# Packing each expert's weights into one transfer, with a new interleaving of the steps, in an eight-image pipeline on one core

## The chip, the core and the metric

The kernel runs on one core of a Trainium2 chip, in one launch. The metric is the device time in microseconds (us). Five engines work side by side, each through its own program: TensorE (PE in the profile; PEld is its weight load), VectorE (DVE), ScalarE (ACT), GpSimd (POOL) and SyncE (SP), which here issues the plain transfers. They wait for each other by counting semaphores, which the program sets and reads explicitly.

## What is computed

Eight images of 32 x 32 tokens and 128 channels, all in fp32, go through six layers with a residual each:

```
x = x + deformable_conv(group_norm(x))       # 9 taps, 4 corners each, gathered at computed places
x = x + sort_over_tokens(corr(group_norm(x)))[ranks]   # 1024 x 1024 correlations, 128 ranks of the sorted row
t = t + windowed_attention(layer_norm(t))    # windows of 4, 16 and 32
u = layer_norm(t)
t = t + u + sum_e g[:, e] * (gelu(u @ w1[e] + b1[e]) @ w2[e] + b2[e])   # 8 experts of 128 x 128, top 2
t = t + state_space_scan(layer_norm(t))
u = layer_norm(t)
h = silu(u @ w1[e].T) * (u @ w3[e].T)        # 8 experts, hidden size 341, top 2
t = t + sum_e g[:, e] * (h @ w2[e].T)
```

The experts are computed for all tokens, and the gate g is zero where a token does not use one. The experts of 128 x 128 are called moe1, those with hidden size 341 moe2 or the last layer.

## The kernel before

**Pipeline.** A body of the program works on several images at once: the first part (F: group norm, deformable convolution with its gathers, correlations) of image i+1, the sort (S, VectorE alone) of image i, and the rest of the layers (C: attention, moe1, scan; M: moe2) of images i-1 and i in halves of 512 tokens. The bodies are called fill, early, full, late and drain by what runs in them; there are six full bodies (i = 1 to 6), and in the drain only C and M are left.

**Order.** Each engine's program is one interleaving of the generators F, S, C and M. The function weave (L1697) goes through a string of letters and lets the generator of that letter write its next step. There is one string for each engine and kind of body in ORDER (L44 and on), `DVE_full`, `PE_full` and so on. A step's instructions stand in the engine's queue where its letter stands, so a letter moved is an instruction moved ahead of or behind others, whatever is ready first.

**Gathers.** pool_F (L748 to L761) issues the gathers of a deformable convolution in groups of three indirect DMAs (L758) into one of two halves of `gath`; group g is issued when the matmuls of group g-2 have freed its half. The matmuls (L597) take 12 gathered 128 x 128 tiles times diagonal weights; each fp32 matmul appears twice in the trace, so 12 instructions are x24 there. L604, L605 and L607 are the convolution proper of a finished tile of 128 tokens (residual, bias, 9 taps).

**Sort.** Comparison stages on 128 x 1024 values twice (L791 and L793 among others), and at the end the selection stages (L901), which keep only the ranks that are wanted; L910 adds the result.

**moe1.** SyncE's sp_C (L956 to L965) loads w1 and w2 of an expert with two DMAs of 64 KB into one of three slots of `e1w`; TensorE's pe_moe1 (L1179 to L1205) waits for them. The layer norm behind it starts with the statistics at L933.

**Scan.** L1316, L1317 (decays), L1332, L1334, L1338 (TensorE's products of a chunk), L1516 (VectorE takes the result), L1344 and L1350 (transposes and output projection), L1530 (VectorE adds it to `tm`).

**moe2.** sp_M (L1537 to L1553) loads an expert's weights with five DMAs into one of two slots of `e2w`: w1 and w3 whole, and w2 in three tiles of 128, 128 and 85 rows. Expert e may be loaded when all of e-2 has been used (`y2_ps`). On TensorE (pe_M) an expert is 3 tiles of its hidden size, 128, 128 and 85. Each tile has u @ w1 (L1605, with `mu_t`), (g u) @ w3 (L1610, with `gated_u`), and, a tile later, the product with w2 (L1590). L1581 makes the gated input of the next expert. ScalarE takes the silu of L1605's result (L1658), VectorE multiplies it with L1610's (L1690), and L1590 uses that. Two banks (MB) alternate between the results, so TensorE can be only about one result ahead of its readers.

## Time and profile before

| | us |
|---|---|
| timed runs | 4749.79, 4736.45, 4748.96; median 4748.96 |
| the profiled execution | 4740.47 |
| its span, first to last instruction | 4738.7 |

Engines over the span: TensorE busy for 3969.3 us (84%) in 20178 instructions, VectorE 4160.9 us (88%) in 5173, ScalarE 3082.4 us (65%) in 7523, GpSimd 940.8 us (20%) in 580. TensorE's granted clock is 0.916 of the full one on average. The chain of work that ended last is 48% VectorE, 34% TensorE, 7% issue, 4% ScalarE, 4% DMA and 3% GpSimd. DMA moves 269.67 MB, 57 GB/s on average.

To read it: fill and early last until 959 us, the six full bodies until 4157 us (each about 532 us), the late body until 4440 us and the drain until the end. Busy shares over the whole span mix these; a stretch is read by its own rows. An idle time in front of an instruction is printed behind it with the engine, tile and line that ended it.

### The profile page before, as it was taken

How to read it: one execution, taken by the hardware profiler on the slowest of the kernel's cores; microseconds unless marked ns; L12 is line 12 of the kernel's file. 1: busy time of each engine (PE TensorE's matmuls, PEld its weight loads, DVE VectorE, ACT ScalarE, POOL GpSimd, SP SyncE). 2: the span in 40 equal slices, each digit the busy share in tenths (PEclk: the TensorE clock that was granted, in tenths of full speed). 3: DMA queues.
4: the chain of work that ended last, by engine and by line, in shares of the span. 5: the costliest groups of instructions: out<-in, count | busy, mean ns of one | idle time of the engine just before them, and what ended most of it. 6: DMA issues, size and time to landing. Idle time of an engine off the chain costs nothing.

```text
span 4738.7 us, 57761 instructions
## 1 busy us (share of the span) xinstructions
PE 3969.3 (84%) x20178; PEld 2730.7 (58%) x20178; DVE 4160.9 (88%) x5173; ACT 3082.4 (65%) x7523; POOL 940.8 (20%) x580
## 2 busy tenths in 40 slices
PE   5756648989889998988989998989889998768787
PEld 3636434676557754676557755676557755544554
DVE  1099999999999999999999999999999999999421
ACT  4536526777668856777668856777568856455562
POOL 2327000341006300351005400341005300000000
PEclk8878869999999999999999999999999999888898
DMA  4323101232023311232013211232023210000001
GB/s 139 102 56 116 29 0 31 73 95 60 19 58 101 86 33 32 76 93 59 19 51 107 83 36 26 75 96 62 20 56 103 86 28 19 18 21 24 28 28 32
DMA packets 227492, 269.67 MB, mean 57 GB/s; under 512 B 27900, under 2 KB 189956, under 8 KB 227076
## 3 DMA queue, kind: packets, MB, share of 16 engines
q0 software_dynamic: 46080, 151.03, 11.0%
q1 hardware_dynamic: 181124, 114.95, 8.6%
q8 instruction: 162, 2.65, 0.2%
q14 instruction: 126, 1.03, 0.1%
HBM read 242.54 MB, written 23.34 MB: 56 GB/s over the span
## 4 chain that ended last, share of the span: by engine, by line
DVE 48%; PE 34%; issue 7%; ACT 4%; DMA 4%; POOL 3%; SPq 1%; DVEq 0%; POOLq 0%; ACTq 0%
PE bank L597 9%; DVE srt_b L846 4%; DVE srt_b L830 4%; DVE srt_a L791 3%; DVE srt_a L793 3%; PE bank L1610 3%; PE bank L1605 3%; DMA gath<-quads,idx 3%; PE bank L1590 3%; POOL gath L758 3%; DVE srt_a L868 3%; DVE srt_b L793 3%; DVE srt_a L858 3%; DVE srt_a L866 2%; DVE act L1690 2%
## 5 line engine op out<-in xcount | busy, mean ns | idle before, releaser
L758 POOL DMA_INDIRECT gath<-quads,idx x576 | 940.6, 1633 | 2844.3 <-DVE idx L722 1942.4
L597 PE MATMUL bank<-diag,gath 128*128 128x128 f32 x4608 | 610.9, 296 | 149.4 <-DMA gath<-quads,idx 149.3
L639 ACT ACTIVATE diag<-ident,w 128x128 f32<-128x128 f32 x2304 | 703.4, 394 | 27.3 <-DVE w L737 27.2
L597 PEld LDWEIGHTS bank<-diag,gath 128*128 128x128 f32 x4608 | 594.7, 211 | 187.9 <-DMA gath<-quads,idx 165.9
L1590 PEld LDWEIGHTS bank<-e2w,act 128*128 128x128 f32 (+1 forms) x3072 | 426.7, 205 | 172.3 <-issue 169.3
L1610 PE MATMUL bank<-gated_u,e2w 128*128 128x512 f32 (+1 forms) x768 | 434.9, 650 | 91.3 <-DVE act L1690 88.7
L1605 PE MATMUL bank<-mu_t,e2w 128*128 128x512 f32 (+1 forms) x768 | 432.6, 647 | 73.9 <-DMA e2w<-moe_w_t 54.0
L1690 DVE TENSOR_TENSOR act<-act,bank 128x512 f32<-128x512 f32 (+1 forms) x384 | 261.0, 680 | 196.4 <-PE bank L1610 163.1
L1590 PE MATMUL bank<-e2w,act 128*128 128x128 f32 (+1 forms) x3072 | 428.7, 288 | 1.5 <-DVE act L1690 1.5
L830 DVE TENSOR_TENSOR srt_b<-srt_a 128x1024 f32<-128x1024 f32 (+3 forms) x208 | 370.8, 1783 | 2.8
L1658 ACT ACTIVATE act<-bank 128x512 f32<-128x512 f32 (+1 forms) x384 | 228.5, 595 | 207.0 <-PE bank L1605 202.8
L846 DVE TENSOR_TENSOR srt_b<-srt_a 128x1024 f32<-128x1024 f32 x192 | 350.6, 1826 | 0.0
L1658 ACT ACT_TABLE_LOAD x223 | 286.1, 1283 | 6.4 <-PE bank L1590 2.6
L1610 PEld LDWEIGHTS bank<-gated_u,e2w 128*128 128x128 f32 (+1 forms) x768 | 132.3, 191 | 248.7 <-issue 236.5
L791 DVE TENSOR_TENSOR srt_a<-srt_b 128x2048 f32<-128x2048 f32 x112 | 256.0, 2286 | 0.8
L793 DVE TENSOR_TENSOR srt_a<-srt_b 128x2048 f32<-128x2048 f32 x112 | 255.8, 2284 | 0.0
L672 ACT ACTIVATE cols<-bank 128x384 f32<-128x384 f32 x192 | 92.0, 483 | 250.4 <-PE bank L597 242.0
L791 DVE TENSOR_TENSOR srt_b<-srt_a 128x2048 f32<-128x2048 f32 x96 | 219.5, 2286 | 1.1
L793 DVE TENSOR_TENSOR srt_b<-srt_a 128x2048 f32<-128x2048 f32 x96 | 219.2, 2283 | 0.0
L866 DVE TENSOR_TENSOR srt_a<-srt_b 128x2016 f32<-128x2016 f32 (+1 forms) x96 | 211.6, 2204 | 0.6
L868 DVE TENSOR_TENSOR srt_a<-srt_b 128x2016 f32<-128x2016 f32 (+1 forms) x96 | 211.7, 2205 | 0.0
L1605 PEld LDWEIGHTS bank<-mu_t,e2w 128*128 128x128 f32 (+1 forms) x768 | 122.8, 189 | 137.8 <-DMA e2w<-moe_w_t 67.0
(339 smaller groups left out, 8101.5 us busy)
## 6 DMA issues: line engine op xcount, KB each, us to landing
e2w<-moe_w_t SPq DMA_DIRECT2D x256, 170.5 KB
quads<-xn_tok SPq DMA_DIRECT2D x128, 128.0 KB, 2.5
e1w<-L_ffn_w SPq DMA_DIRECT2D x256, 64.0 KB
e2w<-moe_w_t SPq DMA_DIRECT2D x256, 64.0 KB
gath<-quads,idx POOLq DMA_INDIRECT x576
e2w<-moe_w_t SPq DMA_DIRECT2D x128, 42.5 KB
x_tok<-x SPq DMA_DIRECT2D x8, 512.0 KB, 4.0
out<-tm SPq DMA_DIRECT2D x16, 256.0 KB, 2.5
```

The costliest lines, as they stand in the source:

```text
L597: ins = T.matmul(FB[q % 2][:, k * P:(k + 1) * P], gath[:, g % 2, k, s * C:(s + 1) * C], diag[:, g % 2, 4 * k + s], start=(s == 0), stop=(s ...
L639: ins = SC.activation(diag[:, g % 2, n], ident[:], ACT.Copy, scale=w[:, n:n + 1])
L758: pool.indirect_dma_start(gath[:, g % 2, k], None, quads, bass.IndirectOffsetOnAxis(idx[:, TG * g + k:TG * g + k + 1], 0)).then_inc(sem["g ...
L791: V.tensor_tensor(dst[:, :, 0:size // 2], lo, hi, ALU.max)
L793: return V.tensor_tensor(dst[:, :, size // 2:size], lo, hi, ALU.min)
L830: V.tensor_tensor(out_lo, lo, hi, ALU.max)
L846: link.put(V.tensor_tensor(out_hi, lo, hi, ALU.min))
L1590: ins = T.matmul(MB[2][:, t * P:(t + 1) * P], act2[0:m, n % ACT2_SLOTS, t * P:(t + 1) * P], e2w[0:m, e % 2, W2 + k * C:W2 + (k + 1) * C], ...
L1605: T.matmul(MB[r % 2][0:m, :], e2w[:, e % 2, k * P:k * P + m], mu_t[:], start=True, stop=True).then_inc(sem["m_ps"], 1)
L1610: T.matmul(MB[r % 2][0:m, :], e2w[:, e % 2, W3 + k * P:W3 + k * P + m], gated_u[:], start=True, stop=True).then_inc(sem["m_ps"], 1)
L1658: SC.activation(act2[0:m, n % ACT2_SLOTS], MB[r % 2][0:m, :], ACT.Silu).then_inc(sem["m_sb"], 1)
L1690: V.tensor_tensor(act2[0:m, n % ACT2_SLOTS], act2[0:m, n % ACT2_SLOTS], MB[r % 2][0:m, :], ALU.mult).then_inc(sem["hh"], 1)
```

## The change

Three things change together.

The weights of a moe1 expert lie side by side in one array `moe1_w_t` (8 x 128 x 256) and come with one DMA of 128 KB instead of two of 64 KB. The weights of a moe2 expert lie in one array `moe2_w_t` (8 x 128 x 1066, w1, w3 and w2 with its last tile filled up to 128 rows by zeros) and come with one DMA of 533 KB, 4264 bytes for each of 128 partitions, instead of five with 511.5 KB together. The semaphores that count them go up by 16 an expert instead of 32 and 80. Slots, and the points from which a load may start, stay.

The strings of ORDER are new for the early, full, late and drain bodies, for all engines. The steps themselves are the same. In the changed file the lines of moe2 carry numbers that are 5 lower (L1600, L1605, L1585 and L1576 for L1605, L1610, L1590 and L1581; L1685 for L1690), those of the scan 1 lower (L1343 and L1349 for L1344 and L1350, L1529 for L1530).

```diff
@@ ORDER, one line of a table of some seventy @@
     SP_full=(
-        "CCCMMCMCCCCFFCCCMMMMMMMMMCCCCMCMFMMMM"
+        "CCCMMMFCCFCCCCCCMMMMMMMMMCMCCCCMMFMMM"
     ),
@@ semaphores @@
-            e1_in0=96, e1_in1=96, e1_in2=64, logit=1, ...
+            e1_in0=48, e1_in1=48, e1_in2=32, logit=1, ...
-            e2_in0=80 * 4, e2_in1=80 * 4, gate_diag=E8, ...
+            e2_in0=16 * 4, e2_in1=16 * 4, gate_diag=E8, ...
@@ sp_C @@
-                sp.dma_start(e1w[:, e % E1_SLOTS, 0], A["L2_ffn_w1"][e]).then_inc(sem["e1_in%d" % (e % E1_SLOTS)], 16)
-                sp.dma_start(e1w[:, e % E1_SLOTS, 1], A["L2_ffn_w2"][e]).then_inc(sem["e1_in%d" % (e % E1_SLOTS)], 16)
+                sp.dma_start(e1w[:, e % E1_SLOTS].rearrange("p a c -> p (a c)"), A["moe1_w_t"][e]).then_inc(sem["e1_in%d" % (e % E1_SLOTS)], 16)
@@ pe_moe1 @@
-                    pe.wait_ge(sem["e1_in%d" % (n % E1_SLOTS)], unit("e1_in%d" % (n % E1_SLOTS), i, h, 32 * (n // E1_SLOTS + 1)))
+                    pe.wait_ge(sem["e1_in%d" % (n % E1_SLOTS)], unit("e1_in%d" % (n % E1_SLOTS), i, h, 16 * (n // E1_SLOTS + 1)))
@@ sp_M @@
-                sp.dma_start(e2w[:, e % 2, 0:HID], A["moe2_w1_t"][e]).then_inc(sem["e2_in%d" % (e % 2)], 16)
-                sp.dma_start(e2w[:, e % 2, W3:W3 + HID], A["moe2_w3_t"][e]).then_inc(sem["e2_in%d" % (e % 2)], 16)
-                for k, m in enumerate(HTILES):
-                    sp.dma_start(e2w[0:m, e % 2, W2 + k * C:W2 + (k + 1) * C],
-                                 A["moe2_w2_t"][e, k * P:k * P + m]).then_inc(sem["e2_in%d" % (e % 2)], 16)
+                sp.dma_start(e2w[:, e % 2], A["moe2_w_t"][e]).then_inc(sem["e2_in%d" % (e % 2)], 16)
@@ pe_M @@
-                        pe.wait_ge(sem["e2_in%d" % (e % 2)], unit("e2_in%d" % (e % 2), i, h, 80 * (e // 2 + 1)))
+                        pe.wait_ge(sem["e2_in%d" % (e % 2)], unit("e2_in%d" % (e % 2), i, h, 16 * (e // 2 + 1)))
@@ layouts @@
+    w2 = np.zeros((E8, len(HTILES) * P, C), np.float32)
+    w2[:, 0:HID] = a["L3_ffn_w2"].transpose(0, 2, 1)
+    w2 = w2.reshape(E8, len(HTILES), P, C).transpose(0, 2, 1, 3).reshape(E8, P, len(HTILES) * C)
+    packed = np.concatenate([a["L3_ffn_w1"].transpose(0, 2, 1), a["L3_ffn_w3"].transpose(0, 2, 1), w2], 2)
```

**TensorE in a full body, around the eighth expert of moe2 for the first half.** `gated_u,e2w` and `mu_t,e2w` are the two products of a tile, `diag,gath` a gather group, `e2w,act` the product with w2, `cols` the convolution. Before:

```order
L597 MATMUL bank<-diag,gath 128x128 x12
L1605 MATMUL bank<-mu_t,e2w 128x512
L1610 MATMUL bank<-gated_u,e2w 128x512
L1590 MATMUL bank<-e2w,act 128x128 x4
L597 MATMUL bank<-diag,gath 128x128 x12
L1605 MATMUL bank<-mu_t,e2w 128x512
L1610 MATMUL bank<-gated_u,e2w 128x512
L1590 MATMUL bank<-e2w,act 128x128 x4
L1605 MATMUL bank<-mu_t,e2w 85x512
L597 MATMUL bank<-diag,gath 128x128 x12
L1610 MATMUL bank<-gated_u,e2w 85x512
```

After, from the end of the first tile on:

```order
L1605 MATMUL bank<-gated_u,e2w 128x512
L1585 MATMUL bank<-e2w,act 128x128 x4
L1600 MATMUL bank<-mu_t,e2w 128x512
L604 MATMUL bank<-x_tok,ident 128x128
L605 MATMUL bank<-conv_bias,ident 128x128
L607 MATMUL bank<-conv_w,cols 128x128 x9
L597 MATMUL bank<-diag,gath 128x128 x12
L1343 MATMUL bank<-ident,arena 128x128 x8
L1605 MATMUL bank<-gated_u,e2w 128x512
L1585 MATMUL bank<-e2w,act 128x128 x4
L1600 MATMUL bank<-mu_t,e2w 85x512
L1349 MATMUL bank<-w_out,arena 128x128 x8
```

Behind these stand L597 x24 (two gather groups) and the last tile's L1605 (85x512). The convolution and the first of the three gather groups, which stood ahead of the expert's first tile, now stand behind it, with the scan's transposes and projection between the second tile's and the third's.

**VectorE at the same place.** `act<-act,bank` is the product of a tile; `srt_a`, `srt_b` are the sort's buffers. Before:

```order
L1690 TENSOR_TENSOR act<-act,bank 128x512
L791 TENSOR_TENSOR srt_b<-srt_a 128x256x8
L793 TENSOR_TENSOR srt_b<-srt_a 128x256x8
L1690 TENSOR_TENSOR act<-act,bank 128x512
L901 TENSOR_TENSOR srt_a<-srt_b 128x4x53x4
L901 TENSOR_TENSOR srt_a<-srt_b 128x4x75x4
L1690 TENSOR_TENSOR act<-act,bank 85x512
L933 BN_STATS mst<-tm 128x6 x4
L941 BN_AGGR mmv<-mst 128x2 x4
L901 TENSOR_TENSOR srt_b<-srt_a 128x4x11x2
```

After, from the second tile's product to the third's (the first tile's stands seven rows above these):

```order
L1685 TENSOR_TENSOR act<-act,bank 128x512
L901 TENSOR_TENSOR srt_a<-srt_b 128x4x53x4
L901 TENSOR_TENSOR srt_a<-srt_b 128x4x75x4
L901 TENSOR_TENSOR srt_b<-srt_a 128x4x11x2
L901 TENSOR_TENSOR srt_b<-srt_a 128x4x42x2
L901 TENSOR_TENSOR srt_b<-srt_a 128x4x43x2
L901 TENSOR_TENSOR srt_b<-srt_a 128x4x32x2
L901 TENSOR_TENSOR srt_a<-srt_b 128x4x11
L901 TENSOR_TENSOR srt_a<-srt_b 128x4x21 x2
L901 TENSOR_TENSOR srt_a<-srt_b 128x4x22
L901 TENSOR_TENSOR srt_a<-srt_b 128x4x21 x2
L901 TENSOR_TENSOR srt_a<-srt_b 128x4x11
```

The third tile's product (L1685, 85x512) stands right behind these: it follows three selection stages now and one before. Between the first tile's product and the second's there are now two pairs of comparisons (L791, L793) and the projection's sum (L1529), where there was one pair.

**TensorE in a full body, where the scan of the first chunk meets the gathers.** Before:

```order
L1590 MATMUL bank<-e2w,act 128x128 x4
L1332 MATMUL bank<-arena,ident 128x256
L1334 MATMUL bank<-arena 128x32 x8
L1338 MATMUL bank<-carry,arena 128x256
L1605 MATMUL bank<-mu_t,e2w 128x512
L597 MATMUL bank<-diag,gath 128x128 x12
L1610 MATMUL bank<-gated_u,e2w 128x512
L1590 MATMUL bank<-e2w,act 128x128 x4
L597 MATMUL bank<-diag,gath 128x128 x12
```

After:

```order
L1605 MATMUL bank<-gated_u,e2w 128x512
L1585 MATMUL bank<-e2w,act 128x128 x4
L1600 MATMUL bank<-mu_t,e2w 85x512
L597 MATMUL bank<-diag,gath 128x128 x12
L1315 MATMUL bank<-future_h,ident_h 128x512
L1316 MATMUL bank<-tbu,later 128x512
L1315 MATMUL bank<-future_h,ident_h 128x512
L1316 MATMUL bank<-tbu,later 128x512
L1331 MATMUL bank<-arena,ident 128x256
L1333 MATMUL bank<-arena 128x32 x8
L1337 MATMUL bank<-carry,arena 128x256
```

The products of the scan's first chunk (L1332 to L1338 before, L1331 to L1337 now) stood behind one gather group of the image and stand behind three now.

## Rows read from the trace of the kernel before

**Rows 1.** Windows: busy us (and instructions) of each engine, three stretches.

```profile
1491.40:2023.00 531.60, 482.38 (x2523) 333.47 (x2522) 517.69 (x646) 385.74 (x943) 121.36 (x72) 0.95 0.22 62
4640.00:4738.70 98.70, 74.85 (x323) 47.40 (x322) 14.41 (x21) 23.67 (x52) 0.00 (x0) 0.88 0.12 35
4695.50:4709.50 14.00, 10.83 (x45) 6.62 (x46) 2.06 (x3) 3.55 (x8) 0.00 (x0) 0.87 0.13 37
```

The columns are the stretch, its length, the busy time of PE, PEld, DVE, ACT and POOL, then the granted clock, the busy share of the DMA engines and GB/s.

**Rows 2.** Waits of VectorE, 959 to 4157: us in total, times, longest.

```profile
DVE act L1690 <- PE bank L1610: 43.5, 16, 7.3
...
DVE msd L1676 <- ACT msd L1622: 5.3, 6, 1.0
DVE lnst L933 <- ACT td L1236: 1.3, 4, 0.4
```

**Rows 3.** Timeline, 1470 to 1506, by engine: start us, us, what, idle before.

```profile
1484.75 1.12 DVE L1530 SCALAR_TENSOR_TENSOR tm<-bank,rms,td 128x128 f32<-128x128 f32 x4
...
1490.18 0.68 DVE L1690 TENSOR_TENSOR act<-act,bank 128x512 f32<-128x512 f32 x1
...
1495.79 2.35 DVE L901 TENSOR_TENSOR srt_a<-srt_b 128x848 f32<-128x848 f32 x2
1504.83 0.68 DVE L1690 TENSOR_TENSOR act<-act,bank 85x512 f32<-85x512 f32 x1 [6.69 <-PE bank L1610]
...
1477.58 2.17 PE L607 MATMUL bank<-conv_w,cols 128*128 128x128 f32 x18
...
1481.37 2.84 PE L597 MATMUL bank<-diag,gath 128*128 128x128 f32 x24
...
1484.91 1.02 PE L1610 MATMUL bank<-gated_u,e2w 128*128 128x512 f32 x2
...
1498.29 5.49 PE L597 MATMUL bank<-diag,gath 128*128 128x128 f32 x24 [4.44 <-DMA gath<-quads,idx]
...
1485.01 0.94 POOL L758 DMA_INDIRECT gath<-quads,idx  x1 [4.35 <-PE bank L597]
1486.26 4.83 POOL L758 DMA_INDIRECT gath<-quads,idx  x1 [0.30 <-issue]
1491.39 4.70 POOL L758 DMA_INDIRECT gath<-quads,idx  x1 [0.30 <-issue]
```

**Rows 4.** Waits of TensorE, 4640 to 4738.7.

```profile
PE bank L1605 <- DMA e2w<-moe_w_t: 20.3, 6, 3.8
```

**Rows 5.** Timeline, 4718 to 4726, SyncE's issues (SPq) and TensorE.

```profile
4718.88 0.33 SPq L1542 DMA_DIRECT2D e2w<-moe_w_t  x1
...
4719.73 1.28 SPq L1545 DMA_DIRECT2D e2w<-moe_w_t  x3
...
4722.83 2.08 PE L1605 MATMUL bank<-mu_t,e2w 128*128 128x512 f32 x2 [3.15 <-DMA e2w<-moe_w_t]
...
4724.70 1.67 PE L1610 MATMUL bank<-gated_u,e2w 128*128 128x512 f32 x2
```

**Rows 6.** The page's DMA issues: count, KB each, median us to landing.

```profile
x_tok<-x SPq DMA_DIRECT2D x8, 512.0 KB, 4.0
out<-tm SPq DMA_DIRECT2D x16, 256.0 KB, 2.5
```

**Rows 7.** Timeline of TensorE behind two shorter waits.

```profile
771.17 1.10 PE L1605 MATMUL bank<-mu_t,e2w 128*128 128x512 f32 x2 [2.14 <-DVE act L1690]
...
2466.49 1.98 PE L1610 MATMUL bank<-gated_u,e2w 128*85 128x512 f32 x2 [2.17 <-DVE act L1690]
```

**Rows 8.** Timeline of VectorE behind rows 3: the two small selection stages.

```profile
1506.54 1.42 DVE L901 TENSOR_TENSOR srt_b<-srt_a 128x88 f32<-128x88 f32 x4
1507.99 1.49 DVE L901 TENSOR_TENSOR srt_a<-srt_b 128x44 f32<-128x44 f32 x7
```

**Rows 9.** Timeline of GpSimd at the third gather group of an image.

```profile
1956.56 1.41 POOL L758 DMA_INDIRECT gath<-quads,idx  x1 [8.10 <-PE bank L597]
...
1960.41 2.90 POOL L758 DMA_INDIRECT gath<-quads,idx  x1 [0.31 <-issue]
```

More of the change, by code:

```diff
@@ L74 @@
     ),
     SP_full=(
-        "CCCMMCMCCCCFFCCCMMMMMMMMMCCCCMCMFMMMM"
+        "CCCMMMFCCFCCCCCCMMMMMMMMMCMCCCCMMFMMM"
+    ),
+    DVE_full=(
+        "CMSSCMSSSSSMSSMSSSCCMSSCCMSSMSSSMSSSSSSCSSSCMSSMSSCMFCFCSSCFMCSSCFMSSSSSMSSSSMSSSSMSSSSSSSSSCMSS"
+        "CSSMSSSSSSSSSCSSCMSSCMSSCFSSCFMCCFFMSSCFSSSCMSSCSSMSSCMSSSSCCMSSCSSCMSSCMSSCMSSSSCMSSCSSCMSSSMMS"
+        "SSCMSSSCSSMSSMSSSMSSMSSCCMSSSCMCSSSSSSSSSSSCMSSCMSSMSSCSSSCMSSCMSSCMSSCSSCMSSMSSSSSMSSSSMSSSSSSM"
+        "SSSCMSSCSSSSMSSSSCSSCMSSCSSSCMSSCMSSCCMSSCFFMCFSSCFMSSFSSCMSSCMSSCSSCMSSCMSSCMCSSCSSCSSCSS"
@@ new lines @@
+        "MFMCFMMMCCMFFFMFFFFFFMFCMMCMFFFFFFCCMCFFFCMCCFMMFFFCMCFFFMFFFFFMMFCCFFFCFMFFFFFFFFMMFFFMCFMCFFFM"
+        "CFFCCCFFCFFFCCCMCCFMFFCFMCFFFCFMMFFFCFMFCFFMCFFMCMMFFFFFFMFFFMFFFFFFMFFMMCCMCCMCCCCMCCCCCCCCMMCM"
+        "CMCFFFFCMCCFFMMCFCCFFCCCCCCCCMCFMFMFMMMFCCMFMFMMFCCMFFCCMCFMCMCMCFCCFMFCCFCFFFFF"
+    ),
+    SP_late=(
+        "CCCMMMCMCCCCCCCMMMMMMMMCCMCCCMMMMM"
+    ),
+    ACT_late=(
+        "MCFFFMCMFCCCMCFCFFCCFCCFFCMCCCMMFCMMCFMFCMCMMMMMMMMCCMCCMCCCCMCCCCCCCCMMCMCMCCMCMMCCCCCCCCCCCCMM"
+        "CMMMMCCMMMMCCMCCMCCMCMCCMCCCCMMMMCCMCCCCCCCCCMCCCCMMCMMCCMCMMMMMMCCMCCMMCMCCCCCMMCCCCCCMMCMCMCCM"
+        "CCMMCCCCCCCCCCCMMCMMMMCCMMMMCCMCCMCMCMCMCCCMCCC"
@@ L115 @@
+        "MSSCSSSSSMSSSSSSCSSCMSSCMSSCSSSCMSSCCMSSCMSSCSSCMSSSSCMSSCMSSCSSCCSSMSSCCMSSCSSCMSCSMSMSSSCSSCMS"
+        "SSMSSMSSSCCMSSCCMSSMSSSSSSSSSCSSSCMSSMSSCSSCMSSCSSSCMSSCMSSCMSSSSMSSSSSMSSMSSSSMSSSSMSSCMSSSCSSS"
+        "SMSSSSCSSCMSSCMSSCSSSCMSSCCMSSCMSSCSSCMSSSSCMSSCMSSCSSCMSSCMSSCMCSSCSSCSSSCS"
     ),
     DVE_drain=(
-        "MCMCMMMMMMCCMCCMCMCMMCCCCCCMMMMMMCMCCCMMCMCCCCCCMCMCMCCCMCMCCMCCMMCMMMMMMMMMMMMMMMMMMMMMMMMMMMMM"
+        "MCMCMMMMMMCCMCMMCMMCMCCCCCCCMMMMMCMCCCMCMMCCCCCCCMCMMCCMMCCMCCMCCMCMMMMMMMMMMMMMMMMMMMMMMMMMMMMM"
@@ L323, in build @@
             expd=2, probd=2, prob_ps=2, prob_sb=2, ctx_ps=1, ctx_sb=1, att_out=1, t1=1,
-            e1_in0=96, e1_in1=96, e1_in2=64, logit=1, g_e=1, g_exp=1, gated=1, gt_ps=1, gt_sb=1, h_ps=E8, gelu=E8, gy=E8, y1_acc=E8,
+            e1_in0=48, e1_in1=48, e1_in2=32, logit=1, g_e=1, g_exp=1, gated=1, gt_ps=1, gt_sb=1, h_ps=E8, gelu=E8, gy=E8, y1_acc=E8,
             y1_ps=E8, t2=1,
@@ L1842, in layouts @@
         w_out_t=t(a["L3_attn_W_out"].T.reshape(2, P, C).transpose(1, 0, 2)),
-        moe2_w1_t=t(a["L3_ffn_w1"].transpose(0, 2, 1)), moe2_w3_t=t(a["L3_ffn_w3"].transpose(0, 2, 1)),
-        moe2_w2_t=t(a["L3_ffn_w2"].transpose(0, 2, 1)),
+        moe1_w_t=t(np.concatenate([a["L2_ffn_w1"], a["L2_ffn_w2"]], 2)), moe2_w_t=t(packed),
   )
```

62 lines of the change are left out of this document (21 added, 41 removed).

## Prediction

> **What bounds the kernel now.** I read the stretches first. A middle body of the pipeline lasts 531.6 us, and VectorE is busy for 517.7 us of it, TensorE for 482.4 us [rows 1]. So VectorE sets the pace of the six full bodies, and only 13.9 us of each can be won; the sorting and the other VectorE work is not touched by the change. In the last 98.7 us it is the other way round: VectorE is busy for 14.4 us, TensorE for 74.9 us [rows 1], and the chain goes load, matmul, evacuation, product. These are the two places where the change can act.
>
> Next the waits of VectorE in the full bodies. One group stands out: the product of an expert of the last layer (L1690) waits for TensorE's L1610, 43.5 us in 16 waits, the longest 7.3 us [rows 2]. That is one wait of about 6.7 us in each of the six full bodies and little else. The next group is 5.3 us in 6 waits, 0.9 us a body [rows 2]. The timeline shows what it is made of [rows 3]. TensorE has done the matmuls of one gather group at about 1484.2. That frees the buffer, and GpSimd issues the three indirect DMAs of the group after the next: 0.94 us, then 4.83 and 4.70 us, each beside a pair of long VectorE comparisons. The data are there at 1498.29, the 24 matmuls take 5.49 us because TensorE has stood still and its granted clock is down, and only behind them comes the L1610 on which VectorE has waited since about 1498.1. From freed buffer to VectorE's product it is 1504.8 - 1484.2 = 20.6 us, and VectorE had 13.9 us of other work to cover it.
>
> Last the waits of TensorE in the last stretch: 20.3 us in 6 waits for the load of the expert's weights [rows 4]. Each expert needs its own load, the slot is free only when the expert before the last is done, and nothing else is left to run.
>
> **The change, part by part.**
>
> Fewer issues. An expert of the last layer costs SyncE one issue instead of five, one of moe1 one instead of two. SyncE waits nearly all the time, and in the full bodies the loads are under VectorE's work, so the saved issues give nothing there by themselves: 0 us. The one bigger transfer moves 533 KB instead of 511.5 KB (zeros pad the last tile), which the DMA engines, 13% busy in the sixth expert's cycle [rows 1], don't feel.
>
> The last stretch. Now the first issue starts at 4718.88, the third kind, three issues in 1.28 us, at 4719.73, so the very last issue at about 4720.7, and TensorE goes on at 4722.83 [rows 5]: 3.95 us from the first issue, of which 1.8 us pass until the last issue and 2.1 us from there. This wait is 3.15 us and the mean of the six 3.4 us, so the mean from first issue to matmul is 4.2 us. With one transfer the 1.8 us of issuing go, but all the data then stand behind one issue. Upper bound: 2.1 us and all of the data behind it; the share of the DMA engines in the sixth expert's cycle, 0.13 of 14.0 us, says 1.8 us for 16 engines [rows 1], so 3.9 us. Lower bound: 256 KB land 2.5 us after their issue; 512 KB land after 4.0 us, though among the gathers of a full body [rows 6]. I take 3.4 us, nearer to the middle of the two since part of the 2.1 us is the tail of the earlier transfers. That is 0.8 us for each of six loads: **-4.8 us** (0.3 to 1.7 us each, so -1.8 to -10). The Trainium skill, "DMA: Bandwidth & Descriptors", "Anatomy of one DMA", fits 2.0 us plus bytes over 436 GB/s for one DMA from the GpSimd path, which is an estimate of 3.25 us here and would give 0.95 us each, 5.7 us in all; the trace agrees with its fixed part (2.1 us for the 42.5 KB at the end).
>
> Then the clock. Behind such a wait of 3.15 us the next matmuls run at half clock: L1605 takes 2.08 us and L1610 1.67 us [rows 5] where they take 1.02 us otherwise [rows 3], 1.7 us lost for each load. The wait would become 2.6 us on average. Behind waits of 2.14 and 2.17 us the clock held once (1.10 us) and fell once (1.98 us) [rows 7], so I count a fifth of 6 x 1.7 us: **-2 us**, from 0 to -10.
>
> The rest of the drain, 4440 to 4640, where the experts of the first half run beside the scan of the second: TensorE waits for scalars and the scan and hardly for weights. The new order groups moe1's experts more tightly there. I give it **-2 us**, and 8 us either way, because a step moved by one tile costs or gives about one tile (2.6 us) and there are a few of them.
>
> The wait in the full bodies. The order moves both sides of it (the pieces of TensorE and VectorE above). On VectorE the last product now stands behind the two small selection groups, 1.42 and 1.49 us [rows 8], so it is wanted 2.9 us later. On TensorE the convolution and the first of three gather groups now stand behind L1605 of the first tile and not ahead of it, so the buffer is freed later: about 0.9 for the products, 0.9 for the next gate, 2.4 for the convolution and 2.7 for the gather's matmuls, 6.9 us behind the first tile's L1605 (L1610 before the change), which ends 4 to 5 us ahead of its product on VectorE (1485.9 against 1490.18, [rows 3]); so some 2 us behind that product. From that product VectorE now has 16.5 us of work to the last one (four comparisons of 2.2 us, the projection's 1.1 us, two products of 0.6 us and 5.3 us of selection), where it had 8 us. That leaves 14.5 us of cover for what took 20.6 us, against 13.9 us. So 0.6 us is sure if the gather takes as long as now. It may be quicker, since its third DMA now falls beside selection and not beside comparisons; without any blocking three issues take under 4 us instead of 11.1 us, and the half clock of 5.49 us may go too. I take 2.5 us of the 6.7 us in each of six bodies: **-15 us**, between -40 (the wait is gone) and 0.
>
> The Trainium skill, "SBUF — State Buffer", "SBUF: two separate sides", says that the ports shared by VectorE and GpSimd are an exclusive lock, and that descriptors written by GpSimd starve while VectorE holds it. By it the length of the comparisons and not the DMA sets the 4.8 us, which the rows bear out (4.83 and 4.70 beside comparisons, 0.94 else); the new order keeps those comparisons in front of the gather, and if both middle DMAs stayed blocked the term above would be 6 times 0.6, -4 us.
>
> New waits. Beside the big wait VectorE waits for little more than 1 us in most full bodies [rows 2], so the old order fitted; the new one moves some hundred steps. The tightest that I find: moe1's eight experts have to run in about 38 us of VectorE's work where they had 47 us before (my sum of the rows between the gates and the next statistics; TensorE's rows in it sum to 35 us), and the wait of the statistics (L933) for it is 1.3 us in 4 waits now [rows 2]. A second is the projection (L1530): TensorE's L1350 for it now stands behind 12 us of matmuls after the first tile's gate, and VectorE asks for it 9.5 us after the first tile's product, which leaves 2 us. I take **+8 us** for six bodies, 0 to +40 for its range.
>
> Sum: -4.8 - 2 - 2 - 15 + 8 = -16 us. The profiled execution took 4740.5 us (span 4738.7 us and 1.8 us around it), so it would be 4724.5 us. The three timed runs lie at 4736.5, 4749.0 and 4749.8 us; the profiled one is 8.5 us under their median. I put the base in the middle, 4744.7 us, and forecast **4728 us**. Against the runs a difference of 0.3% (14 us) is about what can be told from no change.
>
> **The rivals.**
>
> A gather that blocks the scan (slower). In the new order the third gather group of an image stands ahead of TensorE's L1332 to L1338 for the first chunk, whose result VectorE wants at L1516; in the old one it stood behind them. Its DMAs take 1.41 to 2.90 us each now, done 7 us after their start [rows 9], and then the new order has some 2 us of slack by my sums. If they are blocked as those of rows 3 were, 11 us instead of 7, VectorE waits 2 us, and with the half clock behind it 5 to 6 us. It decides from a delay of 2 us. Six bodies give +33 us on top of the forecast without its +8: 4744.7 - 24 + 33 = 4754 us at least, and 4765 us if the old wait stays as well. For it: the same lock. Against it: at that place GpSimd ran at 1.4 to 2.9 us in the old order.
>
> The middle doesn't move. The gather's blocking and the new waits cancel what VectorE's new cover gives, and only the last 100 us get better: -5 to -9 us, 4738 us. For it: the cover grows by only 0.6 us if the gather stays as slow.
>
> The wait goes. The gather is issued between the comparisons, all six waits of 6.7 us go (-40 us), and the drain gives 8 more: 4697 us. For it: the product is wanted 2.9 us later; against it: the chain was 6.7 us late.
>
> The packed load is no faster. If 533 KB behind one issue take the upper 3.9 us or more, the last stretch gives 0 to 2 us. Then the whole is at 4736 us.
>
> **How the numbers follow.** Forecast (middle gains 4 to 12 us, drain the rest): 43%. Middle unmoved: 24%. Wait gone: 13%. Blocked scan: 14%. Load no faster: 6%. Faster by over 0.3%: three quarters of the forecast and the case without the wait, 46%. Slower by over 0.3%: the blocked scan and a little of the middle case, 17%. Within: 37%. The range leaves out the far ends of the two extreme cases, 4696 to 4764 us.
>
> **What would show it.** One SyncE issue per expert, and TensorE's waits for weights in the last stretch at 2.6 us instead of 3.4 us, six of them; L1605 behind them at 2.08 us or 1.1 us tells the clock term. VectorE's wait for the last tile's gated product: 4 us instead of 6.7 us in each full body, with GpSimd's DMAs just ahead of it. VectorE busy for the same 517.7 us in a body whose length drops from 531.6 to about 530 us. The forecast is wrong if a wait of VectorE for the scan's product, or for moe1's output, of some us shows in each body; or if the load takes as long as before.

## The result and the profile after

The changed kernel is slower: 4798.1 us (median of four runs, 4793.0 to 4802.1) against 4743.8 us of the kernel before (median of four, 4736.5 to 4749.8). The ratio is 1.012, with a 95% interval of 1.0102 to 1.0139, so +54 us where the prediction said -16 us. The profiled execution took 4802.1 us, span 4800.3 us.

Where the time went is read from stretches first. A middle body, from one add of the ranks (L910) to the same add a body later, and the last 98.7 us, in windows of the changed kernel (stretch, length, busy time of PE, PEld, DVE, ACT, POOL, granted clock, DMA share, GB/s):

```profile
2064.74:2606.80 542.06, 484.03 (x2525) 333.95 (x2524) 518.17 (x646) 380.07 (x937) 130.99 (x73) 0.95 0.21 61
...
4701.60:4800.30 98.70, 78.51 (x338) 49.34 (x338) 15.79 (x23) 26.40 (x59) 0.00 (x0) 0.89 0.12 36
```

VectorE has as much to do as before (518.2 us against 517.7 us in [rows 1]), and the body is 10.5 us longer. Five of the six bodies read alike: 542.3, 540.3, 542.1, 542.7 and 542.6 us. From the adds of the ranks, the six bodies together take 3239.4 us where they took 3185.3 us: 54.1 us, with 52.4 us of it idle time of VectorE and 1.7 us busy time. The front grew by 4.9 us and the end by 2.6 us, which makes the 61.6 us between the two spans.

What VectorE waits for in the middle, 959 to 4200 us of the changed kernel (us in total, times, longest):

```profile
DVE act L1685 <- ACT act L1653: 46.5, 6, 7.8
DVE arena L1515 <- PE bank L1337: 28.1, 10, 4.4
DVE arena L1113 <- PE bank L1004: 14.9, 5, 3.2
DVE arena L1510 <- ACT arena L1421: 5.6, 5, 1.1
DVE lnsd L1052 <- ACT lnsd L1042: 3.7, 6, 0.6
DVE act L1685 <- PE bank L1605: 2.1, 6, 0.8
```

The old wait is gone altogether: the last group fell from 43.5 us to 2.1 us [rows 2]. The place that rows 3 showed reads now, on the timeline (start us, us, what, idle before):

```profile
2594.46 2.09 POOL L758 DMA_INDIRECT gath<-quads,idx  x1 [0.30 <-issue]
...
2601.14 2.95 PE L597 MATMUL bank<-diag,gath 128*128 128x128 f32 x24 [0.47 <-DMA gath<-quads,idx]
...
2605.05 0.68 DVE L1685 TENSOR_TENSOR act<-act,bank 85x512 f32<-85x512 f32 x1
```

No DMA of GpSimd stands for 4.8 us there, TensorE waits 0.47 us for the gather instead of 4.44 us, its matmuls take 2.95 us instead of 5.49 us, and VectorE's last product starts on time. But five groups of waits stand above it now, four of them of 5 us or more. Of these four the old list had one of over 0.2 us, and that in a single body. The largest, at the first product of an expert:

```profile
2155.22 5.25 POOL L758 DMA_INDIRECT gath<-quads,idx  x1 [0.30 <-issue]
...
2155.64 2.84 PE L597 MATMUL bank<-diag,gath 128*128 128x128 f32 x24
2165.27 5.49 PE L597 MATMUL bank<-diag,gath 128*128 128x128 f32 x24 [6.79 <-DMA gath<-quads,idx]
2170.55 1.25 PE L1600 MATMUL bank<-mu_t,e2w 128*128 128x512 f32 x2
...
2172.35 0.58 ACT L1653 ACTIVATE act<-bank 128x512 f32<-128x512 f32 x1
...
2172.96 0.69 DVE L1685 TENSOR_TENSOR act<-act,bank 128x512 f32<-128x512 f32 x1 [7.82 <-ACT act L1653]
```

It is the old wait over again at another place. The twentieth gather group stands right behind the nineteenth and ahead of the expert's L1600. GpSimd's DMA stands for 5.25 us, TensorE waits 6.79 us for the data and then runs at half clock for 5.49 us, ScalarE's silu comes after both, and VectorE waits 7.82 us. The second place, at the scan's result:

```profile
2531.79 1.02 PE L1600 MATMUL bank<-mu_t,e2w 128*85 128x512 f32 x2
2537.68 5.49 PE L597 MATMUL bank<-diag,gath 128*128 128x128 f32 x24 [4.87 <-DMA gath<-quads,idx]
...
2547.39 0.69 PE L1337 MATMUL bank<-carry,arena 32*128 32x256 f32 x2
...
2524.61 4.60 POOL L758 DMA_INDIRECT gath<-quads,idx  x1 [0.31 <-issue]
2529.52 5.80 POOL L758 DMA_INDIRECT gath<-quads,idx  x1 [0.30 <-issue]
...
2548.12 0.42 DVE L1515 TENSOR_TENSOR arena<-bank,ecum 128x256 f32<-128x256 f32 x1 [4.12 <-PE bank L1337]
```

This is the rival of the blocked gather as the prediction described it: the third group ahead of the scan's first products, its last two DMAs of 4.6 and 5.8 us, half clock behind the wait. With the two waits that follow from it, 1.5 us at the next chunk's L1515 and 1.1 us at L1510, it costs 6.7 us a body. The list has it for five bodies; in the first full body it stands before 959, at 923 to 934, again 6.7 us, and so is in what the front grew by. The third is small:

```profile
2086.37 0.58 ACT L1059 ACTIVATE u_t<-bank 128x512 f32<-128x512 f32 x1
...
2087.00 3.78 PE L989 MATMUL bank<-u_t,wqkvo 128*128 128x512 f32 x4 [3.32 <-ACT u_t L1059]
...
2097.00 1.16 DVE L1113 TENSOR_TENSOR arena<-bank,band 128x960 f32<-128x960 f32 x1 [2.56 <-PE bank L1004]
```

ScalarE copies the attention's input late (behind the copy of a late gather group, four diagonals and a table load), and TensorE's chain to the scores is late by 2.6 to 3.2 us.

In the last stretch the loads went nearly as forecast: TensorE waits for weights six times, 16.6 us in all. SyncE's issue (SPq) and TensorE, and the page's line for the load:

```profile
4780.84 0.33 SPq L1541 DMA_DIRECT2D e2w<-moe_w_t  x1
...
4784.40 1.12 PE L1600 MATMUL bank<-mu_t,e2w 128*128 128x512 f32 x2 [2.76 <-DMA e2w<-moe_w_t]
4785.36 1.66 PE L1605 MATMUL bank<-gated_u,e2w 128*128 128x512 f32 x2
```

```profile
e2w<-moe_w_t SPq DMA_DIRECT2D x128, 533.0 KB, 3.6
```

From issue to matmul it is 3.56 us, where the five issues took 3.95 us [rows 5] and 4.2 us on average.

### The profile page after: what moved, and what is told of

It is laid out like the page before. It is cut to its first block, busy times and chain, and to the rows that moved or that the text cites. A ratio compares the mean times of both kernels' runs of the same rounds, so it can differ in the third digit from the quotient of the medians.

```text
span 4800.3 us, 57083 instructions
## 1 busy us (share of the span) xinstructions
PE 4007.2 (83%) x20178; PEld 2744.0 (57%) x20178; DVE 4163.3 (87%) x5173; ACT 3038.7 (63%) x7479; POOL 991.8 (21%) x580
## 4 chain that ended last, share of the span: by engine, by line
DVE 45%; PE 33%; issue 6%; ACT 6%; POOL 5%; DMA 4%; SPq 0%; DVEq 0%; POOLq 0%; ACTq 0%
PE bank L597 7%; POOL gath L758 5%; DVE srt_b L846 4%; DVE srt_b L830 4%; DMA gath<-quads,idx 4%; DVE srt_a L858 3%; PE bank L1585 3%; DVE srt_a L868 3%; DVE srt_a L791 3%; PE bank L1605 3%; DVE srt_a L793 3%; DVE srt_a L866 3%; PE bank L1600 2%; DVE act L1685 2%; DVE srt_b L858 2%
## 5 line engine op out<-in xcount | busy, mean ns | idle before, releaser
L758 POOL DMA_INDIRECT gath<-quads,idx x576 | 991.6, 1722 | 2866.6 <-DVE idx L722 1909.2
L597 PE MATMUL bank<-diag,gath 128*128 128x128 f32 x4608 | 630.6, 301 | 187.2 <-DMA gath<-quads,idx 182.4
L597 PEld LDWEIGHTS bank<-diag,gath 128*128 128x128 f32 x4608 | 610.0, 215 | 217.6 <-DMA gath<-quads,idx 196.8
L1585 PEld LDWEIGHTS bank<-e2w,act 128*128 128x128 f32 (+1 forms) x3072 | 419.5, 202 | 166.1 <-issue 164.3
L1600 PE MATMUL bank<-mu_t,e2w 128*128 128x512 f32 (+1 forms) x768 | 427.3, 639 | 70.9 <-DMA e2w<-moe_w_t 43.5
L1605 PE MATMUL bank<-gated_u,e2w 128*128 128x512 f32 (+1 forms) x768 | 434.1, 649 | 58.6 <-DVE act L1685 54.0
L1585 PE MATMUL bank<-e2w,act 128*128 128x128 f32 (+1 forms) x3072 | 423.5, 286 | 0.0
L1685 DVE TENSOR_TENSOR act<-act,bank 128x512 f32<-128x512 f32 (+1 forms) x384 | 261.3, 681 | 182.9 <-PE bank L1605 123.3
L830 DVE TENSOR_TENSOR srt_b<-srt_a 128x1024 f32<-128x1024 f32 (+3 forms) x208 | 370.6, 1782 | 2.6 <-issue 0.3
L1653 ACT ACTIVATE act<-bank 128x512 f32<-128x512 f32 (+1 forms) x384 | 227.6, 593 | 205.3 <-PE bank L1600 202.8
L846 DVE TENSOR_TENSOR srt_b<-srt_a 128x1024 f32<-128x1024 f32 x192 | 350.8, 1827 | 0.0
L1605 PEld LDWEIGHTS bank<-gated_u,e2w 128*128 128x128 f32 (+1 forms) x768 | 134.4, 192 | 226.3 <-issue 202.4
L791 DVE TENSOR_TENSOR srt_a<-srt_b 128x2048 f32<-128x2048 f32 x112 | 256.0, 2286 | 1.1
L793 DVE TENSOR_TENSOR srt_a<-srt_b 128x2048 f32<-128x2048 f32 x112 | 255.8, 2284 | 0.0
L791 DVE TENSOR_TENSOR srt_b<-srt_a 128x2048 f32<-128x2048 f32 x96 | 219.6, 2288 | 0.8
L793 DVE TENSOR_TENSOR srt_b<-srt_a 128x2048 f32<-128x2048 f32 x96 | 219.4, 2285 | 0.0
L1600 PEld LDWEIGHTS bank<-mu_t,e2w 128*128 128x128 f32 (+1 forms) x768 | 122.0, 189 | 130.6 <-issue 61.0
```

The source lines that it names most:

```text
L597: ins = T.matmul(FB[q % 2][:, k * P:(k + 1) * P], gath[:, g % 2, k, s * C:(s + 1) * C], diag[:, g % 2, 4 * k + s], start=(s == 0), stop=(s ...
L758: pool.indirect_dma_start(gath[:, g % 2, k], None, quads, bass.IndirectOffsetOnAxis(idx[:, TG * g + k:TG * g + k + 1], 0)).then_inc(sem["g ...
L791: V.tensor_tensor(dst[:, :, 0:size // 2], lo, hi, ALU.max)
L793: return V.tensor_tensor(dst[:, :, size // 2:size], lo, hi, ALU.min)
L830: V.tensor_tensor(out_lo, lo, hi, ALU.max)
L846: link.put(V.tensor_tensor(out_hi, lo, hi, ALU.min))
```

## The experiments

Every experiment was compared with runs of the kernel before on the same chip; their medians lay between 4734 and 4742 us, and not all experiments ran on one chip, so times of different experiments are compared with care (the intervals of the ratios are 10 to 25 us wide). The names g3, g9, g11, g20 stand for the third, ninth, eleventh and twentieth gather group of an image (of 24).

**The two halves of the change.** One run takes the changed kernel and the old table:

```diff
-ORDER = dict( ... the new strings ... )
+ORDER = dict( ... the strings of the kernel before ... )
```

> The changed kernel with the order strings of the kernel before: the packed loads alone. Theory (the order costs all of the +54 us, the packed loads give a little in the last stretch): TensorE's six waits for weights in the last 100 us sum to about 16.6 us instead of 20.3 us, VectorE keeps its wait of 6.7 us for the last gated product in each full body, periods stay 532 us, and the whole is 3 to 6 us below the kernel before, ratio 0.999. Rival (the packed loads disturb the gathers or the other transfers): periods of full bodies grow by some us and the whole comes out at 4755 us or more.

Measured: 4734.0 us, ratio 0.9987 (0.9977 to 0.9998). VectorE's waits in the middle are nearly those of before (39.9 us in 15 for L1605, and one of 6.6 us for L1653 in two bodies), and the last stretch reads:

```profile
PE bank L1600 <- DMA e2w<-moe_w_t: 16.7, 6, 2.9
```

The packed loads alone give 6.4 us (4740.3 us for the kernel before on that chip), 1 to 11 us by the interval of the ratio: at the edge of what can be measured, as the theory had it. The other run takes the kernel before and the new table:

```diff
-ORDER = dict( ... the strings of the kernel before ... )
+ORDER = dict( ... the new strings ... )
```

> The kernel before with the new order strings: the order alone, five and two loads for each expert. Theory (order): periods of 542 us, VectorE waits 7.8 us for the first silu of an expert (L1658), 5.7 us for the scan's product (L1516) and 3 us for the attention's scores in each full body, the whole at about 4802 us, 4 us over the changed kernel, ratio 1.013. Rival (the packed loads or both together are needed for the loss): below 4760 us.

Measured: 4802.8 us, ratio 1.0137 (1.0121 to 1.0152), with the same waits as the changed kernel (46.4 us, 29.4 us and 15.3 us in the three groups). The order costs all of it, and the transfers are not to blame.

**The ends of the pipeline.** The new strings in the full bodies only:

```diff
-    PE_early=( new ), PE_late=( new ), PE_drain=( new ), ... the same for DVE, ACT and SP
+    PE_early=( old ), PE_late=( old ), PE_drain=( old ), ... the same for DVE, ACT and SP
     PE_full=( new ), DVE_full=( new ), ACT_full=( new ), SP_full=( new ),
```

> The changed kernel with the new strings in the full bodies alone; the early, late and drain bodies have those of the kernel before. Theory (the full bodies carry the loss, the other strings cost some 5 us in the drain): periods of 542 us as in the changed kernel, and the stretch behind the last ranked half takes 317 us instead of 322 us, so the whole is 5 to 10 us below the changed kernel, 4788 to 4793 us. Rival (the new strings of the bodies at the ends gain what was hoped for, and more is lost in the full bodies): the whole is at 4798 us or above.

Measured: 4785.7 us, ratio 1.010 (1.0074 to 1.0126), 12.4 us below the changed kernel, a little more than expected. The stretch behind the last add of the ranks takes 316.7 us, as with the old strings and packed loads (316.9 us), where the changed kernel needs 322.3 us and the kernel before 321.3 us. So the loads give 4.4 us there and the new order takes 5.4 us back. The other traces bear out that there is such a cost beside packed loads (322.2 to 322.5 us with the new strings, 313.0 to 318.7 us with the old), but with the loads of before the new strings cost nothing there (321.6 against 321.3 us). The steps from run to run are -6.4 us for the loads, +51.7 us for the full bodies' order (4785.7 against 4734.0) and +12.4 us for the ends. The second is far outside the noise and the first barely; the last is not settled, since the intervals of the two ratios overlap (1.0102 to 1.0139 and 1.0074 to 1.0126).

**g3 behind the scan.** In the changed kernel one letter of TensorE's string moves, and two of ScalarE's, so that the copy behind g3 doesn't hold the next decay (L1421):

```diff
     PE_full=( ...
-        "...MCMFMMMFCCMMMF..."
+        "...MCMFMMMCCMFMMF..."
     ACT_full=( ...
-        "...MMCMFFFFFFCCMC..."
+        "...MMCMFFFFCFFCMC..."
```

> The changed kernel with one gather group moved: in TensorE's full body the third gather group stands behind the scan's first products and the last gated product instead of ahead of them, and on ScalarE the copy that follows it stands behind the next decay. Theory (TensorE stands still in front of the blocked gather while VectorE waits for the scan): VectorE's waits for the scan (L1515, 5.7 us, and L1510, 1.1 us) fall under 1 us in each full body, the periods fall from 542.3 us to about 535.6 us, the whole from 4798 us to about 4761 us. Rival (the scan's chain itself is late): the wait stays at 4 us or more, the whole stays within 10 us of 4798 us.

Measured: 4753.4 us, ratio 1.0028 (1.0015 to 1.0041): 44.7 us won by one move. The waits in the middle, and the place (timeline):

```profile
DVE act L1685 <- ACT act L1653: 44.1, 6, 7.9
DVE arena L1113 <- PE bank L1004: 9.2, 3, 3.2
...
DVE arena L1515 <- PE bank L1337: 0.8, 1, 0.8
```

```profile
2518.76 0.69 PE L1337 MATMUL bank<-carry,arena 32*128 32x256 f32 x2
2519.38 1.09 PE L1605 MATMUL bank<-gated_u,e2w 128*85 128x512 f32 x2
2520.31 2.84 PE L597 MATMUL bank<-diag,gath 128*128 128x128 f32 x24
...
2505.54 4.61 POOL L758 DMA_INDIRECT gath<-quads,idx  x1 [0.30 <-issue]
2510.45 5.80 POOL L758 DMA_INDIRECT gath<-quads,idx  x1 [0.30 <-issue]
```

GpSimd's DMAs for the group stand just as long (4.61 and 5.80 us). But TensorE has other work meanwhile, reaches the group when its data are there, and so runs it in 2.84 us instead of 5.49 us. The wait and the half clock behind it both go. This is the second place shown: the wait there was nothing but the position of one step. The gain is more than the 40.4 us of the six scan waits less the 1.6 us that is left of them, since the waits for the scores fell too, from 14.9 us to 9.2 us.

**g20 behind the next expert's tiles**, again in the changed kernel:

```diff
     PE_full=( ...
-        "...MMMFMMMFFMMMMCMMCMMCCMM..."
+        "...MMMFMMMFMMMMCMMCMMFCCMM..."
     ACT_full=( ...
-        "...FFFFFFMFFMMCCMCCM..."
+        "...FFFFMMMCCMFFFFCCM..."
```

> The changed kernel with another gather group moved: in TensorE's full body the twentieth gather group stands behind the next expert's three tiles (it stood ahead of them), and its copy and diagonals on ScalarE stand behind the expert's silus. Theory (the 7.8 us that VectorE waits for the first silu is TensorE and ScalarE standing in front of the blocked gather): the wait is gone in all six full bodies and at most 1 to 2 us appear in the second layer's experts behind it, the periods fall from 542.3 us to 535 to 536.5 us, the whole from 4798 us to 4755 to 4765 us. Rival (VectorE waits for weights or for the first expert's chain anyway): the wait stays over 4 us.

Measured: 4801.2 us, ratio 1.0121 (1.0105 to 1.0136): nothing won. The 7.8 us are gone from their place, and VectorE waits 6.6 us at the next expert instead:

```profile
DVE act L1685 <- PE bank L1605: 44.3, 15, 6.6
```

```profile
2173.38 3.61 ACT L639 ACTIVATE diag<-ident,w 128x128 f32<-128x128 f32 x12
2177.00 1.28 ACT L1227 ACT_TABLE_LOAD   x1
2178.30 0.69 ACT L1227 ACTIVATE arena<-bank,b 128x512 f32<-128x512 f32 x1
...
2179.13 1.18 PE L1182 MATMUL bank<-u_t,e1w 128*128 128x512 f32 x2 [2.64 <-ACT arena L1227]
...
2190.78 0.69 DVE L1685 TENSOR_TENSOR act<-act,bank 128x512 f32<-128x512 f32 x1 [6.56 <-PE bank L1605]
```

The twelve diagonals that follow the group on ScalarE (3.61 us) now stand in front of moe1's second gelu, and moe1's chain of product, gelu, product runs without air. The expectation allowed 1 to 2 us for that and was wrong by 5. The wait did leave its place, as the cause that was named has it; the remedy was not one.

**Three moves.** g3 as above, g20 behind two tiles of the expert, its diagonals behind all of moe1, and the attention's copy (L1059) ahead of the four diagonals and the table load:

```diff
     ACT_full: L672 (g20) behind L1213; the 12 L639 of the group behind moe1's last L1221
     ACT_full: L1059 from behind L1626 to right behind L672
     PE_full:  L597 (g20) behind L1585 of the next expert's second tile; L597 (g3) as above
```

> The changed kernel with three moves in the full bodies: the third gather group behind the scan's first products (worth 45 us alone); the twentieth group behind two tiles of the next expert, with its diagonals on ScalarE behind the second layer's experts, so that they delay no gelu; and on ScalarE the copy of the attention's transposed input ahead of four diagonals and a table load. Theory (the three new waits are independent, each the price of one step's place): the wait for the scores goes from 3 us to under 1 us, of the 7.8 us at the twentieth group 3 to 5 us are won since the experts behind it are tight, the whole comes to 4753 - 15 - 25 = 4713 us, 4705 to 4725 us. Rival (the second layer's experts have no air at all in this order): the 7.8 us reappear behind them and the whole is at 4735 us or more.

Measured: 4734.0 us, ratio 0.9974 (0.9961 to 0.9987), 64 us below the changed kernel and as fast as the packed kernel in the old order. It was expected at 4705 to 4725 us, so that was missed; the rival's line was 4735 us. VectorE's waits in the middle are now 17.0 us in 13 for L1605, 11.9 us in 6 for the end of moe1 (L933) and 9.7 us in 12 (L1052). So moving three steps takes back all that the new order lost, but less than the three waits add up to, since moe1 takes some of what is won: 2.0 us a body at L933.

**Does VectorE hold GpSimd off?** The sort's comparisons on one of four tiles (the other three are left unsorted), in the changed kernel and in the kernel before:

```diff
             def runs(buf, m):
-                return buf[:].rearrange("p g (b m) -> p (g b) m", m=m)
+                return buf[:, 0:1].rearrange("p g (b m) -> p (g b) m", m=m)
```

> The changed kernel, in which the comparison stages of the sort work on a quarter of the rows (one of four tiles; the other three are left unsorted), so each comparison of VectorE takes about 0.6 us instead of 2.2 us. Theory (GpSimd's indirect DMAs stand for 4.6 to 5.3 us because VectorE's long comparisons hold them off): the longest ones fall to 2 us or less, their mean from 1.72 us to about 1 us. Rival (the queue or the DMA engines hold them off): indirect DMAs of over 4 us remain. The time falls in any case, to between 3900 and 4400 us, since TensorE is then the bound.

> The kernel before with the same shortening of the sort (the comparison stages work on one of four tiles, the rest is left unsorted). Theory (the new order loses because TensorE's and ScalarE's steps come late for VectorE, at a few places, and not because TensorE's or ScalarE's chains are longer): without VectorE's load both orders take nearly the same time, within 20 us of each other. Rival (the new order makes the chains of the other engines longer): the new order is slower by 50 us or more here too.

Measured, one execution each: 4398.9 us and 4378.2 us. In the changed kernel the longest of 576 indirect DMAs is 2.09 us, where 30 took over 4 us; the mean is 1.02 us instead of 1.72 us. In the kernel before six took over 4 us, one in each body, all at one place:

```profile
1829.94 2.28 DVE L877 TENSOR_TENSOR srt_b<-srt_a 128x2048 f32<-128x2048 f32 x1
1832.14 2.28 DVE L879 TENSOR_TENSOR srt_b<-srt_a 128x2048 f32<-128x2048 f32 x1
...
1830.30 4.94 POOL L758 DMA_INDIRECT gath<-quads,idx  x1 [8.84 <-PE bank L597]
```

L877 and L879 are the pair of comparisons that the edit left at full length, in both kernels. The DMA starts beside the first and ends 0.8 us after the second: a control that was not planned. It isn't the only outcome: in each of the two kernels one DMA starts beside L877 and ends 0.8 us after it (2.02 us), and the next takes 1.90 us beside L879. With VectorE unloaded the two kernels lie 20.7 us apart, just past the line of 20 us that the expectation drew, and far from the rival's 50. So longer chains of the other engines are not the most of the loss. Whether they are a part of it stays open: there is one execution of each, and only one of the two kernels has the packed loads.

**Can the old wait go without new ones?** Packed loads, old order, g9 (the group of rows 3) behind the last gated product and its four products with w2:

```diff
     PE_full=( ...
-        "...MMMFMMMMMFFF..."
+        "...MMMMMMMMFFFF..."
     ACT_full: L1662 and L1617 ahead of L672 (g9) and its diagonals
```

> Packed loads with the order of the kernel before, and one gather group moved in the full bodies: on TensorE the ninth group (the last ahead of the third convolution) stands behind the last gated product and the four last products with w2 of the eighth expert, on ScalarE its copy and diagonals stand behind the output copy and the next layer norm's square root. Theory (VectorE's old wait of 6.7 us is only TensorE standing in front of the blocked gather, and nothing else is late there): the wait is gone in all six full bodies, periods fall from 532 us to about 526 us, the whole from 4734 us to 4694 us (6 x 6.7 us). Rival (as in the run with the twentieth group, the next chain is late instead): the periods stay over 530 us, with a new wait of VectorE of 4 us or more, and the whole stays over 4720 us.

Measured: 4756.0 us, ratio 1.0026 (1.0013 to 1.004), 22 us slower than without the move. VectorE's wait moved on to the router's logits:

```profile
DVE msm L1128 <- PE bank L1557: 45.4, 7, 7.8
...
DVE act L1685 <- ACT act L1653: 13.0, 2, 6.5
```

TensorE stands in front of g11 there, for 4.41 us, and then at half clock. The same again with g11 behind the router's products:

```diff
     PE_full: L597 (g11) behind L1557
     ACT_full: L1042 and L1623 ahead of the 12 diagonals
```

> Packed loads with the order of the kernel before, the ninth gather group moved as in the earlier run, and with it the eleventh: on TensorE it stands behind the router's products of the last layer (L1557) instead of ahead of them, and on ScalarE the next norm's square root and the copy of the transposed input stand ahead of twelve diagonals. Theory (the wait of 7.8 us at the router's logits that the first move brought is again TensorE standing in front of a blocked gather, and VectorE's work covers it at the new place): that wait falls to 1 us or less, the one at L1052 from 1.9 us to under 1 us, periods fall from 532 us to about 525 us, the whole from 4756 us to 4695 to 4710 us, below both kernels. Rival (the gather chain itself has become too long for the stretch, and each move only hands the wait to the next chain): a new wait of 4 us or more behind it, and the whole stays over 4725 us.

Measured: 4755.9 us, ratio 1.0033 (1.0017 to 1.0049). The rival again:

```profile
DVE act L1685 <- ACT act L1653: 41.4, 6, 7.1
DVE arena L1113 <- PE bank L1004: 26.7, 6, 5.6
```

The wait went to the attention's scores and to g20. In this order g20 stands ahead of moe1's first product, and it is late in all six bodies now, in two of them with only g9 moved or with the packed loads alone. The kernel before has that wait once in six bodies, in its list for 959 to 4157:

```profile
DVE act L1690 <- ACT act L1658: 6.7, 1, 6.7
```

Last, every place seen so far at once:

```diff
     PE_full: as above, and L989 ahead of L597 (g12); L597 (g11) behind the transposes of tbu; L597 (g20) behind L1605
     ACT_full: as above, and L947, L1059 ahead of L672 (g11); L672 (g20) behind L1227 and L1653
```

> Packed loads with the order of the kernel before and every step that two earlier runs showed VectorE waiting for moved: the ninth and eleventh gather group as before, on ScalarE the second layer norm's output and its transposed copy ahead of eight diagonals and of the copy behind the blocked gather, on TensorE the attention's projection (L989) ahead of the twelfth group, and the twentieth group behind the next expert's first two products of the last layer, its copy behind the first silu. Theory (each wait is the price of a step's place, and VectorE's air is enough to take the gathers at the new places): the waits of 5.5 us (L1113) and 6.9 us (L1685) fall to 2 us or less each, periods fall from 535.7 us to 527 us or less, the whole from 4756 us to 4710 us or less, below the packed kernel in the old order (4734 us). Rival (a fixed amount of waiting is handed on to the next chain whatever is moved): periods stay at 533 us or more and the whole stays over 4740 us.

Measured: 4706.6 us (median of six, 4703.3 to 4712.1), ratio 0.994 (0.9925 to 0.9956). This beats both kernels, by 28 us against the kernel before on the same chip. Its waits in the middle, and a body:

```profile
DVE act L1685 <- PE bank L1605: 10.8, 19, 2.1
DVE arena L1113 <- PE bank L1004: 6.8, 6, 1.2
```

```profile
2022.73:2551.11 528.38, 480.01 (x2525) 331.03 (x2524) 517.81 (x645) 385.27 (x943) 129.22 (x72) 0.95 0.22 63
```

No wait is longer than 2.1 us. Waits aren't a fixed amount that is handed on for ever: once each long one has work in front of it, what remains is some 11 us a body, of which small gaps between instructions are 5.5 us. The body was expected at 527 us or less and is 1.4 us longer; the whole was expected at 4710 us or less and is at 4706.6 us.

## Why the prediction was wrong

Point by point, by its own steps.

**What bounds.** Right. The loss is VectorE's idle time in the full bodies; its busy time changed by 1.7 us.

**The loads.** Right in mechanism, somewhat too large in size. 3.4 us were taken from issue to matmul and 3.56 us measured, so a load gave 0.6 us where the sum had 0.8 us. With the clock behind it, it gave 0.74 us (13.45 us from one expert to the next in the run with the old order, 14.19 us before), 4.4 us for six, where the sum had 6.8 us (-4.8 - 2). The -6.4 us of the run with the loads alone lie nearer to the sum, but that is the whole kernel, known to 5 us either way. The Trainium skill, "DMA: Bandwidth & Descriptors", "Anatomy of one DMA", has a fit from which the prediction estimated 3.25 us for the transfer; measured are 3.56 us until the matmul, so the estimate is 0.3 us short here.

**The clock behind the loads.** It was to hold in one of five cases. It fell behind every load: L1600 behind the six waits takes 1.99, 1.82, 1.64, 1.41, 1.15 and 1.12 us, and the L1605 behind it 1.9 us five times and 1.66 us the last time, where either takes 1.02 us otherwise. From load to load the fall comes later in the pair. The 1.7 us of loss had been read from one load; in the kernel before, too, L1605 behind the six waits differs, from 1.26 to 2.08 us.

**The old wait.** Sized wrong, in the safe direction: 2.5 us of 6.7 us were taken, and all of it went, 41.4 us in six bodies. The sum had 14.5 us of cover against 20.6 us of gather, and said itself that -40 us was possible. But the 20.6 us were not a constant. With the step moved, GpSimd's three DMAs fall elsewhere beside VectorE's comparisons (the one ahead of it is 2.09 us long and not 4.8 us), and TensorE, which does not stand still, runs at full clock.

**New waits, +8 us.** This is the step that failed. Measured are 46.5 us for L1653, 33.7 us for the scan (28.1 + 5.6) and 14.9 us for the scores, 95 us in the window, and 6.7 us more for the scan in the first full body. The term was put at 8 us, from a reading of the tightest chains by sums of durations, and its range ended at +40. The prediction's own sign of being wrong, a wait of VectorE for the scan's product of some us in each body, is there.

- The scan was named as a rival with the right mechanism and the right price: 5.5 us a body, and 6.7 us measured. The rival was given 14% because GpSimd took 1.4 to 2.9 us at that place in the old order [rows 9]. That duration belonged to where the DMA fell among VectorE's comparisons in the old order and not to the DMA.
- The largest, g20 ahead of the next expert, was not seen. The prediction followed one place at which a gather stood in front of a step that VectorE wants, and there are 24 gather groups in a body. The list of waits had the hint: a wait of 6.7 us on L1658, once in six equal bodies. It was passed over as a single event. It was a step on the edge, caught by GpSimd's block in one body of six, and in the new order in six.
- The chain of moe1 was named as the tightest, at 38 us for 35 us of TensorE's rows. It did not wait by itself (L933 is not in the list of after); that it came 7.8 us late together with VectorE would explain this, and the runs that moved g20 fit: it then cost 6.6 us, and 2.0 us with the diagonals out of its way.

**The rest of the drain, -2 us.** Nothing was won: beside the packed loads the new strings cost 5.4 us behind the last add of the ranks. With the early and the late body it is 12.4 us by the run that left them out, which is not clear of noise. Where exactly was not followed.

**The range.** 4696 to 4764 us held the rivals one at a time. (The scan's rival with the old wait left in place was put at 4765 us; its terms add up to 4769 us, 4744.7 - 24 + 33 + 15. Either lies outside the range.) The result is two of one kind at once and a third: the old wait gone (-41 us), g3 (+40 us), g20 (+46 us less the 6.7 us it had before), the scores (+15 us), the ends (+12 us), the loads (-6 us), in sum +59 us. The medians are 54 us apart and the two profiled executions 62 us, so the sum is no closer than that. The terms were treated as independent, while the blocked gather is one mechanism that acts at every place where TensorE stands in front of it.

## What to carry to other kernels

When an in-order engine feeds several consumers from one program, ask for every step that can be late (here each gather) what stands right behind it in the queue and who wants that; moving the step behind the wanted work cost nothing and gave 45 us, and no engine had to become faster. Look at all places of the kind together: with the waits behind it left as they were, a move that removed its own wait could give nothing or a loss (4801 us against 4798 us, and 4756 us twice against 4734 us), and the moves of g9 and g11 together with those for the waits behind them gave 28 us below the kernel before. And read a wait that appears in one of several equal periods as a step on the edge and not as noise.
